# Second attention: even maxima with a row for two heads at a time, and one value product over high and low parts of the context keys

## The chip, the cores and the metric

The kernel runs on one core of a Trainium2 chip. Its engines are TensorE (PE in the rows; PEld is its loading of weights), VectorE (DVE), ScalarE (ACT), GpSimd (POOL) and SyncE (SP), which here issues nearly all transfers. They run side by side and wait for one another by semaphores. The metric is the device time of one execution in microseconds (us).

## The reference

Two layers run one after the other. The change lies in the attention of the second, in which 512 tokens of a batch (four batches) attend to the same 512 tokens and to 64 keys of a context. Cut to what matters:

```python
h = jnp.concatenate([x, latents], axis=1)            # x: 64 context tokens, latents: 512 tokens
q = (latents @ q_w + q_b).reshape(b, 512, 16, 32)
kv = (h @ kv_w + kv_b).reshape(b, 576, 16, 32, 2)
attn = jnp.einsum('bkhd,bnhd->bhkn', q, kv[..., 0]) / 32
attn = softmax(where(mask, attn, -inf))              # the mask concerns the 64 context keys
attn_out = jnp.einsum('bhkn,bnhd->bkhd', attn, kv[..., 1]) @ out_w + out_b + residual
```

All is float32. The kernel gets this precision from products of high and low parts: a number is split into a rounded high part and the rest, and three products (high by high, high by low, low by high) are added.

## The kernel before

A batch has 16 heads of 32 columns, in four groups of four (`c` is the group, `j` the head in it). The 576 keys of a head are five blocks: `t` 0 to 3 are 128 of the own tokens, `t` 4 (`TT`) is the 64 context keys. So a group has 20 steps (`NSTEP`), one for each (j, t) of `STEPS`, and a batch 80. In step n:

- TensorE multiplies keys by queries (`scores`, L2064) into one of two banks; the keys lie on the partitions, the 512 queries along them. Row 97 of the query stack (`ROWMAX`) holds the negative maximum of each query, so the product comes out with the maximum subtracted.
- ScalarE takes the exponential twice, once into the high part `ph` (L1156) and once in full into `pf` (L1157).
- VectorE or GpSimd (by `lo_by_pool`) writes the low part `pl` = pf - ph (L1331, `lo_p`, or L894).
- Four steps later (`LAG`), TensorE adds the values (`values`, L2079 with `ph` and L2080 with `pl`). The weights are 65 columns: 32 of high values, 32 of low values, one of ones for the sum.

The maxima must be known before a group's scores. TensorE computes the scores of the next group the other way round, queries on the partitions (`max_step`: L2042, or L2046 for the context keys, four small products), into one of two banks, and VectorE reduces each (L1570, L1573) before the bank is used again. `max_items(i)` says which of the 20 belong to step i: all within steps 2 to 15. At step 17 (`TURN`) VectorE joins the maxima of the group's four heads, TensorE turns them (L2053), VectorE copies the row out (L1586), and SP moves it to row 97 (`max_row`, L565). The next group's first scores wait for it (`maxed`).

Between the steps TensorE works off `fillers`: the projections of queries (Q), keys (K) and context keys (KC) of the group after next, and in group 1 also the turning of the next batch's tokens (T0 to T3, C). They and the turned maxima share two banks in a fixed order (`results`). SP moves the projected parts to memory and back into stacks (L546, L557). After step 79 comes a stretch of its own, with the values of the next batch's keys (`nV0` to `nV4`; `nV4` is the context), the sums' inverses and the output product (L2088). Before batch 0 comes a prologue that projects batch 0's values and takes the 20 maxima of its group 0 (`first_max`).

Of the kernel before, what the change touches and what calls it, by code (L numbers as in the profile page):

```python
# [26 lines left out]
F32 = mybir.dt.float32  # L27
# [8 lines left out]
P = 128  # L36
B, S, D = 4, 512, 512
C = 64
# [39 lines left out]
TURN = 17  # L78
OPEN_NORM = 4
# [24 lines left out]
def results(last):  # L104

    out = []
    for c in range(G):
        turn = [(TURN + 0.5, 1, f"R{c + 1}")] if c + 1 < G else [] if last else [(TURN + 0.5, 1, "nR0")]
        out += [u for _, _, u in sorted(fillers(c, last) + turn)]
# [5 lines left out]
         + [f"nV{t}" for t in range(TT)] + ["nR0", f"nV{TT}"])  # L115


def first_max(t, part):

    at = 2 * t + part  # L120
    return range((5 * at + 1) // 2, (5 * (at + 1) + 1) // 2)
# [57 lines left out]
def lo_by_pool(i):  # L179

    j, t = STEPS[i % NSTEP]
    return t in (1, 3) or (t == TT and j % 2 == 0)
# [27 lines left out]
def program(nc, x, ctx, mask_bool, mask_int, w, x1, xm, x2, q_parts, k_parts, out):  # L210
# [4 lines left out]
    with es:  # L215
# [41 lines left out]
        nT = rows_[0:H, 0:2 * P].rearrange("p (s n) -> p s n", s=2)  # L257
# [13 lines left out]
        pl = pl_.rearrange("p (r n) -> p r n", r=PRING)  # L271
        AS = [t[:, 0:TT * KT * P].rearrange("p (r k n) -> p r k n", r=TT, k=KT) for t in (ph_, pl_)]
# [66 lines left out]
        maxed = [sem("maxed0"), sem("maxed1")]  # L339
# [121 lines left out]
        def _(sp):  # L461
# [77 lines left out]
            def attention1():  # L539
# [31 lines left out]
                def batch(b, last):  # L571
# [14 lines left out]
                    for c in range(G):  # L586
# [5 lines left out]
                        def pair(half, xs=(0, 1)):  # L592
                            wait_apart(sp, (s_full, at(0, b, BSTEP, NSTEP * c + 2 * (TT + 1) * (half + 1))))
                            stack(nb, nc_, half, xs)
                        if last and c == G - 1:

                            wait_apart(sp, (pb_full, at(0, b, USES, use1(f"R{G - 1}", last) + 1)),
# [5 lines left out]
                        if c == 2 and not last:  # L603
                            wait_apart(sp, (pb_full, at(0, b, USES, use1(f"nT{KT - 1}") + 1)))
                            residual(b)
                        if ahead:
                            wait_apart(sp, (pb_free, at(0, b, USES, use1(f"{pre}Q{nc_}", last) + 1)))
                            parts(0, nb, nc_)
                        sums(HG * c)
                        if ahead:  # L610
                            pair(0, (0,))
                            wait_apart(sp, (pb_free, at(0, b, USES, use1(f"{pre}KC{nc_}", last) + 1)))
# [1660 lines left out]
```

## Time and profile before

| What | Value |
|---|---|
| median of 3 runs | 1783.35 us (1782.95 to 1785.82) |
| profiled execution, its time | 1778.49 us |
| its span | 1776.7 us |
| PE busy in the span | 1605.4 us (90%) |
| PEld busy | 1202.6 us (68%) |
| DVE busy | 1003.3 us (56%) |
| ACT busy | 688.9 us (39%) |
| POOL busy | 544.1 us (31%) |

The span is what the profiler saw of the program; the execution's own time is 1.8 us longer. Shares of busy time are averages over stages with different limits. A matmul's record is longer than the time after which the next one starts, so costs of TensorE are read here from the distance between two starts.

### The profile page before, as it was taken

Reading aid. Unit: us, or ns where it says so; the run is one execution under the profiler, and the core shown is the slowest. Engines: PE = TensorE matmul, PEld = TensorE weight load, DVE = VectorE, ACT = ScalarE, POOL = GpSimd, SP = SyncE. Lnnn points to the kernel's source line nnn. Section 1 sums busy time; section 2 is a strip of 40 time slices with the busy share of each in tenths; the row PEclk is TensorE's granted clock in tenths of the full one; section 3 lists DMA queues with packets and bytes.
Section 4 is the critical chain, followed back from the end, with each engine's and each line's share of the span. In section 5 each row is a group of like instructions: output and inputs, shape, how many; then the busy total and the mean of one; then the engine's idle time right before and its main releaser. Section 6 shows DMA issues by size and latency. Waiting matters only on the chain.

```text
span 1776.7 us, 23169 instructions
## 1 busy us (share of the span) xinstructions
PE 1605.4 (90%) x7017; PEld 1202.6 (68%) x7017; DVE 1003.3 (56%) x1625; ACT 688.9 (39%) x1243; POOL 544.1 (31%) x543
## 2 busy tenths in 40 slices
PE   5778787899999999798998999899988899999998
PEld 4667676667787787566666566566653677787886
DVE  4665656564333333487857776786788574333333
ACT  3533333341111112176737755773777432111111
POOL 3231236502122231343513432342358311303000
PEclk9888998999999999898999999999897999999999
DMA  5001104500010032522312322332221510101011
GB/s 185 1 33 54 45 28 138 207 13 31 18 30 18 24 133 83 183 77 96 100 59 97 113 67 85 91 101 63 99 88 48 192 52 16 33 12 36 0 48 47
DMA packets 60410, 126.18 MB, mean 71 GB/s; under 512 B 9989, under 2 KB 10378, under 8 KB 60322
## 3 DMA queue, kind: packets, MB, share of 16 engines
q1 hardware_dynamic: 53282, 102.13, 17.4%
q0 software_dynamic: 7040, 23.07, 4.1%
q8 instruction: 31, 0.51, 0.1%
q14 instruction: 57, 0.47, 0.1%
HBM read 90.25 MB, written 34.60 MB: 70 GB/s over the span
## 4 chain that ended last, share of the span: by engine, by line
PE 72%; DVE 13%; issue 7%; ACT 5%; DMA 1%; SPq 1%; POOL 1%; DVEq 0%; ACTq 0%; POOLq 0%
PE bank L2181 19%; PE bank L2193 18%; PE bank L2029 5%; DVE RA L1331 4%; PE bank L2025 3%; PE bank L2079 3%; DVE FA L1570 3%; PE bank L2064 3%; PE bank L2080 3%; PE bank L2088 3%; PE bank L2042 2%; PE bank L1827 2%; PE bank L1851 2%; PE bank L2046 2%; PE bank L1902 1%
## 5 line engine op out<-in xcount | busy, mean ns | idle before, releaser
L2193 PE MATMUL bank<-W,RA 128*128 128x512 f32 x1536 | 378.1, 397 | 6.0 <-DVE RA L1331 5.6
L2181 PE MATMUL bank<-RA,W 128*128 (+1 forms) x1536 | 374.8, 396 | 2.9 <-issue 2.4
L2193 PEld LDWEIGHTS bank<-W,RA 128*128 128x128 f32 x1536 | 286.2, 188 | 77.6 <-DVE RA L1331 10.0
L2181 PEld LDWEIGHTS bank<-RA,W 128*128 128x128 f32 x1536 | 286.9, 188 | 75.1 <-issue 6.1
L894 POOL TENSOR_TENSOR RA<-FA,RA 128x512 fp32r<-128x512 f32 (+1 forms) x160 | 216.6, 1358 | 373.0 <-ACT FA L1157 372.7
L1223 ACT ACTIVATE FA<-bank,cols 128x512 f32<-128x512 f32 x128 | 88.2, 689 | 540.8 <-PE bank L2181 540.7
L1331 DVE TENSOR_TENSOR RA<-FA,RA 128x512 fp32r<-128x512 f32 (+1 forms) x292 | 260.8, 893 | 33.2 <-ACT FA L1157 25.9
L1729 DVE CAST RA<-FA 128x512 fp32r<-128x512 f32 x128 | 62.8, 490 | 357.3 <-ACT FA L1223 357.3
L1156 ACT ACTIVATE RA<-bank 128x512 fp32r<-128x512 f32 (+1 forms) x320 | 193.3, 604 | 165.0 <-PE bank L2064 162.7
L1570 DVE TENSOR_REDUCE FA<-bank 128x1 f32<-128x512 f32 x256 | 168.9, 685 | 63.4 <-PE bank L2042 62.5
L1157 ACT ACTIVATE FA<-bank 128x512 f32<-128x512 f32 (+1 forms) x320 | 192.7, 602 | 0.0
L2064 PE MATMUL bank<-RA 98*128 98x512 f32 (+1 forms) x320 | 139.6, 438 | 9.6 <-ACT FA L1157 5.1
L2079 PE MATMUL bank<-RA 128*65 128x512 f32 (+1 forms) x320 | 138.5, 433 | 7.9 <-DVE RA L1331 4.9
L2029 PE MATMUL bank<-RA,W 128*128 128x512 f32 (+1 forms) x576 | 140.8, 361 | 1.9 <-DVE RA L1331 1.6
L1331 DVE TENSOR_TENSOR RA<-bank,RA 128x512 fp32r<-128x512 f32 (+1 forms) x124 | 83.0, 680 | 95.1 <-ACT RA L951 33.0
L2080 PE MATMUL bank<-RA 128*65 128x512 f32 (+1 forms) x320 | 132.9, 415 | 0.0
L2029 PEld LDWEIGHTS bank<-RA,W 128*128 128x128 f32 x576 | 95.0, 191 | 36.3 <-issue 12.2
L753 POOL TENSOR_TENSOR W<-raw,W 128x512 fp32r<-128x512 f32 (+1 forms) x88 | 108.3, 1231 | 7.3
L2042 PE MATMUL bank<-RA 97*128 97x512 f32 x256 | 96.6, 416 | 13.7 <-issue 6.5
L1764 DVE TENSOR_TENSOR FA<-bank,FA 128x512 f32 (+1 forms) x128 | 86.8, 690 | 38.3 <-PE bank L2193 37.7
L2064 PEld LDWEIGHTS bank<-RA 98*128 98x128 f32 (+1 forms) x320 | 59.3, 185 | 57.1 <-ACT FA L1157 32.6
L749 POOL TENSOR_SCALAR W<-raw 128x512 fp32r<-128x512 f32 (+1 forms) x88 | 57.8, 657 | 109.8 <-PE bank L2193 51.5
(154 smaller groups left out, 1810.2 us busy)
## 6 DMA issues: line engine op xcount, KB each, us to landing
RA<-k_parts SPq DMA_DIRECT2D x96, 144.0 KB
FA<-after_layer SPq DMA_DIRECT2D x12, 1024.0 KB, 5.9
RA<-q_parts SPq DMA_DIRECT2D x96, 128.0 KB
k_parts<-FA SPq DMA_DIRECT2D x16, 576.0 KB, 2.8
after_att<-FA SPq DMA_DIRECT2D x32, 256.0 KB, 2.1
q_parts<-FA SPq DMA_DIRECT2D x16, 512.0 KB, 2.7
raw<-in_L_xattn_mlp_w_dram POOLq DMA_DIRECT2D x32, 256.0 KB, 3.4
RA<-after_att SPq DMA_DIRECT2D x10, 512.0 KB, 7.1
```

The lines of the kernel that those rows point to most:

```text
L894: pool.tensor_tensor(pl[0:m, r, :], pf[0:m, r, :], ph[0:m, r, :].bitcast(F32), ALU.subtract).then_inc(p_lo_pool, 1)
L1156: act.activation(ph[0:m, r, :], src, ACT.Exp, scale=SCALE1)
L1157: act.activation(pf[0:m, r, :], src, ACT.Exp, scale=SCALE1).then_inc(p_exp, 1)
L1331: dve.tensor_tensor(dst, src, hi.bitcast(F32), ALU.subtract).then_inc(sem_, 1)
L1570: dve.tensor_reduce(nm_main[:, TT * j + t:TT * j + t + 1], bank[2 + i % 2][:, :], AX_X, ALU.max, negate=True).then_inc(mm_free, 1)
L2029: op = pe.matmul(dst[:, 0:m], W[:, "QK".index(kind[0]), a, k, c * P:(c + 1) * P], src[:, d, k, :], start=start, stop=stop)
L2042: pe.matmul(bank[2 + i % 2][:, :], QS[0:ROWMAX, c % 2, j, t * P:(t + 1) * P], KS[0:ROWMAX, c % 2, j, 0:S], start=True, stop=True).then_inc ...
L2064: pe.matmul(bank[4 + n % 2][0:m, :], KS[0:ROWMAX + 1, c % 2, j, t * P:t * P + m], QS[0:ROWMAX + 1, c % 2, j, :], start=True, stop=True).th ...
L2079: pe.matmul(o, v, ph[0:m, n % PRING, :], start=(t == 0), stop=False)
L2080: pe.matmul(o, v, pl[0:m, n % PRING, :], start=False, stop=(t == TT)).then_inc(pv_step, 1)
L2181: op = pe.matmul(bank[FC1_BANK[i]][:, :], W[:, slot, a, k, i * P:(i + 1) * P], yT_[:, ds(b * (2 * KT * S) + (d * KT + k) * S, S)], start=( ...
L2193: op = pe.matmul(bank[4 + t][:, :], gs[:, a, i, t * P:(t + 1) * P], W[:, slot + 1, d, i, :], start=(i == 0 and a == 0 and d == 0), stop=(i ...
```

## The change

- **Maxima.** Each step now takes one item: steps 0 to 6 (`SHIFT` is 7) the last seven of the own group, steps 7 to 19 the first thirteen of the next. The row is turned, copied and moved in two halves, each for two heads: heads 0 and 1 at step 17 of the group before, heads 2 and 3 at step 7 of the own group. The first scores of head 0 wait for the one and those of head 2 (step 10) for the other. The last batch's group 2 takes two items a step from step 7 to 16, since group 3 has none. The prologue takes 13 items instead of 20.
- **Fillers.** Q now lies in steps 0 to 5, K in 8 to 13 and KC in 14 and 15 (in group 1: Q 0 to 2, K 3 to 5, KC 8, T at 9, 11, 13 and 15, C at 18).
- **Context values.** The low part of the context's exponentials goes to partitions 64 to 127 of the same slot of `ph` (`lo_place`), and the context's value weights stand twice, on partitions 0 to 63 and 64 to 127. One product over 128 partitions takes the place of two over 64. ScalarE and VectorE have one more instruction each for `nV4`.
- **Who writes low parts.** GpSimd now has t 1 and 3 and, for even heads, t 0 instead of the context block.

```diff
+SHIFT = 7
-def max_items(i):
-    return range(max(i - 2, 0) * 10 // 7, min(max(i - 1, 0) * 10 // 7, NSTEP)) if i < 16 else range(0)
+def max_items(c, i, last):
+    if last and c == G - 1:
+        return []
+    if i < SHIFT:
+        return [(c, NSTEP - SHIFT + i)]
+    if last and c == G - 2:
+        return [(c + 1, 2 * (i - SHIFT) + m) for m in range(2)] if i < TURN else []
+    return [(c + 1, i - SHIFT)]
+def max_turns(c, last):
+    if last and c == G - 1:
+        return {}
+    if last and c == G - 2:
+        return {SHIFT: (c, 1), (SHIFT + TURN) // 2: (c + 1, 0), TURN: (c + 1, 1)}
+    return {SHIFT: (c, 1), TURN: (c + 1, 0)}
...
-    spans = ((1, 5), (6, 5), (11, 1)) if turns else ((1, 6), (7, 5), (12, 1))
+    spans = ((0, 3), (3, 3), (8, 1)) if turns else ((0, 6), (8, 6), (14, 2))
...
-        plan += [(s0, 1, f"nT{k}") for k, s0 in enumerate((12, 13, 15, 18))] + [(19, 1, "nC")]
+        plan += [(s0, 1, f"nT{k}") for k, s0 in enumerate((9, 11, 13, 15))] + [(18, 1, "nC")]
...
-    return t in (1, 3) or (t == TT and j % 2 == 0)
+    return t in (1, 3) or (t == 0 and j % 2 == 0)
...
+        def lo_place(n):
+            return ph[C:P, n % PRING, :] if STEPS[n % NSTEP][1] == TT else pl[:, n % PRING, :]
...
-                def max_row(nb, c):
-                    sp.dma_start(QS[ROWMAX:ROWMAX + 1, c % 2, :, :].rearrange("o j (q n) -> o (j q) n", n=P).bitcast(F32),
-                                 nT[:, c % 2, :].bitcast(F32)).then_inc(maxed[c % 2], 16)
+                def max_row(c, pair):
+                    sp.dma_start(QS[ROWMAX:ROWMAX + 1, c % 2, 2 * pair:2 * pair + 2, :]
+                                 .rearrange("o j (q n) -> o (j q) n", n=P).bitcast(F32),
+                                 nT[:, c % 2, pair, :].bitcast(F32)).then_inc(maxed[c % 2][pair], 16)
...
+                        if t == TT:
+                            act.activation(VP[C:P, t, :, 0:HD], src, ACT.Copy)
...
+                        if t == TT:
+                            dve.tensor_tensor(VP[C:P, t, :, HD:2 * HD], values_, hi_.bitcast(F32), ALU.subtract)
...
-                        if i == 0:
-                            wait_apart(pe, (maxed[c % 2], at(0, b, 32, 16 * (c // 2 + 1))))
+                        if t == 0 and j % 2 == 0:
+                            wait_apart(pe, (maxed[c % 2][j // 2], at(0, b, 32, 16 * (c // 2 + 1))))
...
-                        v = VP[0:m, t, h, 0:2 * HD + 1]
+                        v = VP[:, t, h, 0:2 * HD + 1]
                         o = bank[6 + h % 2][0:2 * HD + 1, :]
-                        pe.matmul(o, v, ph[0:m, n % PRING, :], start=(t == 0), stop=False)
-                        pe.matmul(o, v, pl[0:m, n % PRING, :], start=False, stop=(t == TT)).then_inc(pv_step, 1)
+                        op = pe.matmul(o, v, ph[:, n % PRING, :], start=(t == 0), stop=(t == TT))
+                        if t < TT:
+                            op = pe.matmul(o, v, pl[:, n % PRING, :], start=False, stop=False)
+                        op.then_inc(pv_step, 1)
```

Two places show what moves. The first is TensorE's queue at step 8 of group 0 in the loop over batches 0 to 2. Before, the step has scores (128x512 under L2064), two items of maxima (L2042 and, for the context, four of L2046), the context's values as two products (L2079 and L2080, 65 rows out), and two products of the K filler (L2029):

```order
L2064 MATMUL bank<-RA 128x512
L2040 REGISTER_ALU
L2042 MATMUL bank<-RA 128x512
L2040 REGISTER_ALU
L2046 MATMUL bank<-RA 128x64 x4
L2074 REGISTER_ALU
L2079 MATMUL bank<-RA 65x512
L2080 MATMUL bank<-RA 65x512
L2029 MATMUL bank<-RA,W 128x512 x2
```

In the changed kernel the lines are L2113 (scores), L2090 (maxima), L2127 (values), L2077 (fillers), and L2101 the turning of eight rows of maxima, at the end of step 7:

```order
L2101 MATMUL bank<-ident,FA 8x128
L2111 REGISTER_ALU
L2113 MATMUL bank<-RA 128x512
L2088 REGISTER_ALU
L2090 MATMUL bank<-RA 128x512
L2127 MATMUL bank<-RA 65x512
L2040 REGISTER_ALU
L2077 MATMUL bank<-RA,W 128x512 x2
```

One item of maxima is left in the step, one product in place of two stands for the context's values, and a turning stands ahead of it.

The second place is SP's queue in the same loop, group 0, from the parts of the keys (L546 before) to the row of maxima (L565 before, `RA<-rows_`). Before, a sum (L576) and its wait lie between them:

```order
L546 DMA k_parts<-FA 128x1152
L573 REGISTER_ALU
L576 DMA FA<-FA 1x16x32
L454 REGISTER_ALU
L565 DMA RA<-rows_ 1x16x128
L557 DMA RA<-k_parts 32x2x576 x3
```

Now (L575 the parts, L594 the row, L586 the stack) the half row of step 17 follows the parts at once, since KC ends at step 15 and its parts are ready only then:

```order
L575 DMA k_parts<-FA 128x1152
L483 REGISTER_ALU
L594 DMA RA<-rows_ 1x8x128
L586 DMA RA<-k_parts 32x2x576 x3
```

The row went from behind the sum to right behind the parts of the keys.

## Rows read from the trace of the kernel before

**Rows 1.** Windows of batch 1: groups 0 to 3, then the stretch behind them
```profile
core 0: us, PE busy (x) PEld busy (x) DVE busy (x) ACT busy (x) POOL busy (x), PEclk, DMA share, GB/s
916.45:947.75 31.30, 27.23 (x122) 17.79 (x121) 24.70 (x37) 22.56 (x45) 12.84 (x10) 1.00 0.28 96
947.75:984.66 36.91, 32.67 (x150) 22.21 (x150) 27.21 (x42) 25.92 (x52) 13.83 (x11) 0.95 0.25 76
984.66:1015.92 31.26, 29.09 (x129) 18.90 (x130) 26.56 (x41) 24.28 (x49) 12.99 (x11) 1.00 0.41 124
1015.92:1047.18 31.26, 29.33 (x131) 19.41 (x132) 25.97 (x39) 24.02 (x49) 18.50 (x14) 1.00 0.29 89
1047.18:1080.59 33.41, 31.85 (x129) 21.83 (x128) 17.74 (x24) 7.57 (x13) 2.60 (x2) 1.00 0.21 63
```

**Rows 2.** Windows: prologue's maxima, group 0 of batch 3, group 2 of batch 3
```profile
727.01:747.00 19.99, 18.32 (x79) 14.05 (x77) 12.67 (x22) 1.80 (x3) 4.01 (x5) 0.92 0.47 142
...
1244.62:1277.48 32.86, 29.71 (x122) 19.58 (x121) 24.69 (x37) 22.72 (x45) 12.70 (x10) 0.88 0.26 90
...
1310.10:1340.71 30.61, 25.72 (x93) 14.63 (x94) 24.80 (x36) 23.00 (x46) 24.34 (x24) 0.89 0.31 86
```

**Rows 3.** TensorE's waits in the four batches: us in total, times, longest
```profile
PE bank L2046 <- DVE FA L1570: 22.2, 27, 1.9
PE bank L2006 <- DVE FA L1560: 8.0, 6, 1.6
PE bank L2064 <- DMA RA<-rows_: 4.2, 9, 0.7
```

**Rows 4.** Timeline of TensorE, batch 1, group 0: start, us, instruction [idle before]
```profile
924.06 0.53 PE L2046 MATMUL bank<-RA 97*128 97x64 f32 x4
924.42 0.42 PE L2079 MATMUL bank<-RA 128*65 128x512 f32 x1
...
925.38 0.39 PE L2064 MATMUL bank<-RA 98*128 98x512 f32 x1
...
927.00 0.40 PE L2064 MATMUL bank<-RA 98*128 98x512 f32 x1
...
937.45 1.42 PE L2029 MATMUL bank<-RA,W 128*128 128x64 f32 x12
938.70 0.48 PE L2064 MATMUL bank<-RA 98*128 98x512 f32 x1
939.02 0.64 PE L2042 MATMUL bank<-RA 97*128 97x512 f32 x2
939.59 0.44 PE L2079 MATMUL bank<-RA 64*65 64x512 f32 x1
...
940.18 0.45 PE L2064 MATMUL bank<-RA 98*64 98x512 f32 x1
...
945.01 0.27 PE L2053 MATMUL bank<-ident,FA 128*16 128x128 f32 x1
...
947.75 0.48 PE L2064 MATMUL bank<-RA 98*128 98x512 f32 x1 [0.52 <-DMA RA<-rows_]
```

**Rows 5.** Low parts in batch 1: count, duration in ns min/median/max, span, forms
```profile
L1331 DVE TENSOR_TENSOR RA<-FA,RA x39: 673/723/1773, 919.9 to 1045.9; 128x512 fp32r<-128x512 f32 x32, 64x512 fp32r<-64x512 f32 x7
...
L894 POOL TENSOR_TENSOR RA<-FA,RA x39: 1267/1287/1817, 919.4 to 1045.1; 128x512 fp32r<-128x512 f32 x31, 64x512 fp32r<-64x512 f32 x8
```

**Rows 6.** Transfers: issuer, count, KB each, median us from issue to landing
```profile
k_parts<-FA SPq DMA_DIRECT2D x16, 576.0 KB, 2.8
...
RA<-rows_ SPq DMA_DIRECT2D x22, 8.0 KB, 1.8
```

**Rows 7.** Timeline of the stretch behind batch 1's groups: context values, output
```profile
1067.76 0.59 ACT L1137 ACTIVATE RA<-bank 64x512 fp32r<-64x512 f32 x1 [0.64 <-PE bank L2025]
1068.38 0.68 DVE L1331 TENSOR_TENSOR RA<-bank,RA 64x512 fp32r<-64x512 f32 x1 [0.48 <-ACT RA L1137]
...
1069.31 11.45 PE L2088 MATMUL bank<-W,RA 128*128 128x512 f32 x48 [0.61 <-DVE RA L1331]
```

More of the change, by code:

```diff
@@ L107, in results @@
     for c in range(G):
-        turn = [(TURN + 0.5, 1, f"R{c + 1}")] if c + 1 < G else [] if last else [(TURN + 0.5, 1, "nR0")]
+        turn = [(i + 0.5, 1, turn_name(*of)) for i, of in max_turns(c, last).items()]
         out += [u for _, _, u in sorted(fillers(c, last) + turn)]
@@ L338, in program @@
         stacked = [[sem(f"stacked{i}_{j}") for j in range(2)] for i in range(2)]
-        maxed = [sem("maxed0"), sem("maxed1")]
+        maxed = [[sem(f"maxed{i}_{a}") for a in range(2)] for i in range(2)]
         mm_full = sem("mm_full")
@@ L609, in batch @@
                         sums(HG * c)
+                        if (SHIFT + TURN) // 2 in turned:
+                            turned_row((SHIFT + TURN) // 2)
                         if ahead:
                             pair(0, (0,))
+                        sums(HG * c + 1)
+                        if ahead:
                             wait_apart(sp, (pb_free, at(0, b, USES, use1(f"{pre}KC{nc_}", last) + 1)))
                             parts(1, nb, nc_)
[L614 to L618 removed]
+                        if TURN in turned:
+                            turned_row(TURN)
                         if ahead:
@@ L1633, in batch @@
                         at_step = {s0 + n + 1: u for s0, n, u in fillers(c, last)}
-                        ahead = not (last and c == G - 1)
-                        nb, nc_ = (b, c + 1) if c + 1 < G else (b + 1, 0)
+                        turns = max_turns(c, last)
                         for i in range(NSTEP):
                             n = NSTEP * c + i
-                            if ahead:
-                                for m in max_items(i):
-                                    max_step(nb, nc_, m)
-                                if i == TURN - 1:
-                                    max_join(nb, nc_)
+                            for of, m in max_items(c, i, last):
+                                max_step(b + of // G, of % G, m)
+                            if i + 1 in turns:
+                                of, pair = turns[i + 1]
+                                max_join(b + of // G, of % G, pair)
                             lo_p(n - 1)
@@ L1645, in batch @@
                                 lo(b, at_step[i], last)
-                            if ahead and i == TURN:
-                                max_turned(b, f"R{nc_}" if c + 1 < G else "nR0", nb, nc_, last)
+                            if i in turns:
+                                of, pair = turns[i]
+                                max_turned(b, turn_name(of, pair), b + of // G, of % G, pair, last)
                             h, t = divmod(n - LAG - 2, TT + 1)
@@ L1705, in attention1 @@
                         dve.memset(VP[:, :, :, 2 * HD:VW].bitcast(F32), 1.0).then_inc(consts, 1)
-                for t in range(TT):
+                for t in range(TT - 1):
                     for i in first_max(t, 0):
@@ L1712, in attention1 @@
                         max_step(0, 0, i)
-                max_join(0, 0)
+                max_join(0, 0, 0)
+                lo(0, f"nV{TT - 2}", first=True)
+                max_turned(0, "nR00", 0, 0, 0, first=True)
+                for part in range(2):
+                    for i in first_max(TT - 1, part):
+                        max_step(0, 0, i)
                 lo(0, f"nV{TT - 1}", first=True)
-                max_turned(0, "nR0", 0, 0, first=True)
                 lo(0, f"nV{TT}", first=True)
@@ L2107, in batch @@
                         at_step = {s0 + part: (u, part, n) for s0, n, u in fillers(c, last) for part in range(n)}
-                        ahead = not (last and c == G - 1)
-                        nb, nc_ = (b, c + 1) if c + 1 < G else (b + 1, 0)
+                        turns = max_turns(c, last)
                         for i in range(NSTEP):
                             scores(NSTEP * c + i)
-                            if ahead:
-                                for m in max_items(i):
-                                    max_step(nb, nc_, m)
+                            for of, m in max_items(c, i, last):
+                                max_step(b + of // G, of % G, m)
                             if NSTEP * c + i >= LAG:
@@ L2119, in batch @@
                                 project(b, u, part, n, last)
-                            if not ahead and i >= 17:
+                            if last and c == G - 1 and i >= 17:
                                 spread_inverse(i - 17)
-                            if ahead and i == TURN:
-                                max_turn(b, f"R{nc_}" if c + 1 < G else "nR0", nb, nc_, last)
+                            if i in turns:
+                                of, pair = turns[i]
+                                max_turn(b, turn_name(of, pair), b + of // G, of % G, pair, last)
                     values(BSTEP - 4)
```

58 lines of the change are left out of this document (33 added, 25 removed).

## The prediction

> **What bounds the kernel now.** I read the windows first, cut where each group's first scores start. An ordinary group of 20 steps takes 31.3 us, group 1, which also turns the next batch's tokens, 36.9, and the stretch behind the groups 33.4 [rows 1]. In the windows of the groups TensorE is the busiest engine, but VectorE is close behind it, with 24.7 to 27.2 us; ScalarE has 22.6 to 25.9 and GpSimd 12.8 to 18.5. Since a matmul's record overlaps the next, I then took TensorE's own need from distances between starts [rows 4]:
>
> - A product over 512 columns: from the scores at 925.38 to those at 927.00 lie seven, 1.62 us, so 0.232 each.
> - The four small products of a context maximum: 924.06 to 924.42, 0.36. KC's twelve: 937.45 to 938.70, 1.25. The turned row: 0.27.
> - The context's two value products: two full products start at 939.02 and should end the stretch after 0.46, but the next starts at 939.59, so 0.11 are lost at the change to 64 rows; then 0.59 pass to 940.18. Together 0.70 us for what 128 rows would do in 0.46.
>
> An ordinary group has 92 full products (20 scores, 16 maxima, 32 of values, 24 fillers), 21.3 us, and 4 x 0.36 + 4 x 0.70 + 1.25 + 0.27 = 5.8: 27.1 us. It takes 31.3, so TensorE stands still for 4.2. The list of waits says for what: mostly for a bank of maxima that VectorE has not reduced (22.2 us in 27 waits over the four batches), in group 1 for the bank in which a filler is turned (8.0), and for the row (4.2) [rows 3]. So the stage is bound by TensorE, plus bunched maxima: up to two items in a step for which VectorE must find time between low parts, and none in steps 16 to 19. The chain of waits is alternately TensorE and VectorE for that reason, and neither is idle long.
>
> **The change, part by part.**
>
> *One product for the context values.* It takes 0.232 instead of 0.70, so 0.47 less a head, 1.9 a group, and TensorE's need falls from 27.1 to 25.3; the second turned row brings it to 25.5. For the other bound: if what costs at 64 rows did not vanish with the form, only one product of 0.232 would go, 0.9 a group.
>
> The Trainium skill ("TensorE: Matmul & The Clock Gate", section "Why this matters for your kernels") says that a product over few rows takes the same time as one over 128. By that rule the gain would be the one product, 0.23 a head. The trace disagrees so far: 0.59 us for two.
>
> *Even maxima.* They take nothing off any engine; they remove waits. VectorE's need stays what it was, about 25 to 26.5 us a group, since busy times of 24.7 to 26.6 [rows 1] hold the same instructions, and a second joining and copying add about 0.4. With one item a step, steps with a filler need on TensorE 6 x 0.232 = 1.39 and the six without one (6, 7, 16 to 19) 0.93, where VectorE needs its average of about 1.3. The sum is TensorE's 25.5 plus 6 x 0.37 = 2.2, or 27.7. Not all low parts are alike: one on VectorE takes 0.67 at best and 1.77 at worst, beside GpSimd's 1.29 [rows 5], so a step is now and then late; I add 0.7. And the rows, next, 0.6. An ordinary group then takes 29.0 us, 2.3 less than now. The bounds of this: 26.3 (TensorE's need and 0.8 of waits) and 30.5 (VectorE as slow as now in three of four waits).
>
> *The row in two halves.* From the turning at 945.01 to the scores at 947.75 pass 2.74 us, of which TensorE waited 0.52 [rows 4]; the transfer is 1.8 of them [rows 6]. At step 17 nothing changes in this path but its neighbours: SP now issues the 576 KB of key parts right ahead of the row, and these land after 2.8 us [rows 6]. If a transfer waits for the one in front of it, the row lands about 0.5 to 0.9 later; if not, as now. Steps 18 and 19 give 1.6 us of TensorE's own work and about 2.5 at VectorE's pace, so about the present 0.5 is waited again. The half of step 7 has steps 8 and 9 with fillers in front of it, 2.55 us or more, so 0 to 0.5. No row found here stands behind a large transfer, so both ends stay for the range. What stands behind the waiting scores is all of TensorE's queue, but VectorE catches up meanwhile, so a wait is not lost whole. I take 0.6 a group for both, 0.5 of which it pays now; the other 0.1 is in the sum.
>
> *Group 1.* Its 36.9 us contain waits for the bank of a turned filler, 1.3 us each on average [rows 3]. K now ends at step 5 and the turnings come at every second step, one use behind the other. Its need is 25.5 plus five turnings of about 0.45, 27.8; with the same additions (eight light steps, 3.0; 1.3 for late steps and rows) 32.1, and I take 32.4 for what is left of bank waits: 4.5 less, three times, 13.5.
>
> *Batch 3.* Groups 0 and 1 are both ordinary there; group 0 takes 32.9 at a granted clock of 0.88 [rows 2], and I take group 1 for its like. I take 3 less for each, 6. Group 2 now has 27 items instead of 20, with two a step in ten steps. It has no fillers and TensorE is not its bound; seven more reductions at 0.6, of which two thirds find room: 1.5 more (0 to 3).
>
> *Prologue.* Twenty maxima and four value projections take 20.0 us [rows 2]. Seven items fewer, each worth about 0.45 on the path (its product, and VectorE's 0.6 where it is waited for): 3 less.
>
> *Context values in weights.* Behind the groups, ScalarE's 0.59 and VectorE's 0.68 for `nV4` are in the path: the output product starts at 1069.31 after waiting 0.61 for just this low part [rows 7]. One more of each, at about 0.5 and 0.6 between starts, moves it by 1.1, and what follows on VectorE (the last scaling) by as much: 3 x 1.1 = 3.3 slower, with nothing to hide it. The last head's context product also lies in this stretch: 4 x 0.47 = 1.9 faster.
>
> *Who writes low parts.* GpSimd has ten a group as before and VectorE ten; nothing on the path.
>
> *Sum.* Nine ordinary groups 20.7, three groups 1 13.5, batch 3 6 - 1.5, prologue 3, the stretches 1.9 - 3.3: 40.3 us faster. The profiled execution's 1778.5 becomes 1738.2; the median of the runs lies 4.9 above that execution, so I forecast 1743.
>
> **The rivals.**
>
> *VectorE and GpSimd become the bound.* A low part on VectorE reads two operands from memory, as GpSimd's does, and its spread from 0.67 to 1.77 [rows 5] looks like one waiting for the other. GpSimd's 12.8 us [rows 1] stay the same while the group gets shorter, so more of VectorE's low parts meet it. Then a group takes 30.2, 1.1 less, group 1 gains 2.5, batch 3 3: 10 + 7.5 + 3 - 1.5 + 2 - 1.4 = 20, 1763. For it speaks that VectorE's 26.6 and TensorE's 25.5 would change places; against it, that VectorE's waits for maxima (the bunching) go too. Chance 0.19.
>
> The Trainium skill ("SBUF — State Buffer", section "SBUF: two separate sides") has this as a rule: the two engines share a pair of ports under an exclusive lock for a whole instruction. By that rule the time would be this rival's.
>
> *The product saves only a product.* 0.23 instead of 0.47 a head: 64 x 0.24 = 15 less gained, 1758. Chance 0.08.
>
> *Waits vanish whole.* Groups at 26.5, 4.8 less, group 1 at 29.5: nine by 2.5 and three by 2.9 more than in my sum, 31 in all, 1712. Against it: light steps are too short for VectorE. Chance 0.08.
>
> *Slower: the rows stand in TensorE's way.* There are now two row paths a group, each of at least 2.2 us from turning to landing, with only two steps to hide it. TensorE's turning also waits for VectorE's joining, in the middle of its queue. If VectorE is a step late (1.3) and the transfer sits behind the key parts (0.9), a half row costs 2 us more than I counted: 28 rows in the groups, 56 us, against 40: 1799. It decides from 1.5 us a row on. Against it: the present row waits 0.5 on average where it waits at all. Chance 0.05.
>
> **How the numbers follow.** My own case, from 1729 to 1757, has 0.60. Case by case: 0.60 at 1743, 0.19 at 1763, 0.08 at 1758, 0.08 at 1712, 0.05 at 1799. The range from 1719 to 1767 leaves out the slower case, most of the 1712 one and the upper edge of the VectorE rival, about 0.15 to 0.2. A measurement of this kernel tells about 0.2% (3.6 us) from no change. Faster by more than that: 0.93; within it: 0.02, from the upper end of the VectorE rival; slower: 0.05.
>
> **What would show it.** In the profile of the changed kernel: an ordinary group at 29 us and group 1 at 32 to 33; TensorE's waits for L1570's successor (L1613) down from 22 us to under 8, those on a filler's bank under 3; waits for the row 4 to 15 us in 20 or more waits; the context value product followed by the next after 0.23 to 0.25 us; the low part's spread as now; the output product about 1.1 us later behind the last `nV4` product; VectorE's busy share in a group near 90%. I am wrong if groups stay above 30.3, if row waits pass 30 us in total, or if waits for low parts in `values` appear.

## The result and the profile after

The changed kernel is slower: 1795.01 us median of 7 runs (1790.78 to 1802.12) against 1781.76 us (1777.9 to 1785.82), a ratio of 1.0083 with a 95% interval of 1.0065 to 1.0101. The forecast, 1743 us and faster, was wrong in sign. The profiled execution took 1798.13 us with a span of 1796.3.

In the changed kernel the scores are L2113, the own maxima L2090 (reduced in L1613), the turning L2101, the joining L1623, the copying of the row L1630, its transfer L594, the values L2127 and L2129, the fillers L2077, the low parts L1372 and L933, the output product L2138. The windows of batch 1, cut as in [rows 1], then group 0 of batch 3 as in [rows 2] and group 1 behind it:

```profile
914.17:946.65 32.48, 26.80 (x121) 18.78 (x119) 22.61 (x39) 23.68 (x46) 13.78 (x10) 0.94 0.26 92
946.65:982.59 35.94, 32.88 (x147) 23.49 (x147) 27.09 (x45) 25.08 (x50) 13.59 (x10) 0.88 0.25 80
982.59:1016.85 34.26, 28.68 (x127) 20.27 (x127) 25.74 (x43) 25.05 (x50) 13.83 (x10) 0.94 0.33 111
1016.85:1048.30 31.45, 28.57 (x127) 20.26 (x128) 24.70 (x40) 23.21 (x45) 17.94 (x14) 0.95 0.23 71
1048.30:1084.75 36.45, 33.36 (x131) 23.19 (x128) 19.88 (x27) 8.25 (x14) 1.73 (x1) 0.95 0.23 74
1256.04:1284.91 28.87, 25.02 (x121) 17.80 (x119) 22.42 (x39) 23.55 (x46) 13.84 (x10) 0.98 0.27 99
1284.91:1321.90 36.99, 30.79 (x126) 21.83 (x127) 25.60 (x41) 24.36 (x47) 13.88 (x10) 0.87 0.24 77
```

Batch 1 takes 170.6 us where it took 164.1. Of these windows only group 0 of batch 3 is at the forecast 29; there the clock is 0.98. In every window of batch 1 the granted clock lies below that of before. Over the four batches (first scores to last) it is 0.92 instead of 0.96. TensorE's waits in the same stretch as [rows 3], us in total, times, longest:

```profile
PE bank L2113 <- DMA RA<-rows_: 20.5, 8, 3.3
PE bank L2101 <- DVE FA L1623: 16.5, 16, 1.3
PE bank L2077 <- DVE FA L1598: 9.3, 11, 1.9
PE bank L2127 <- POOL RA L933: 6.1, 2, 3.8
PE bank L2138 <- DVE RA L1372: 5.7, 3, 1.9
PE bank L2090 <- DVE FA L1613: 4.4, 4, 1.6
```

Most of the waits for bunched maxima are gone, 22.2 us to 4.4 (and 2.9 more for the context's maxima, L1616). In their place stand two that the kernel before hardly had: the row, 4.2 to 20.5 us, in few but long waits, and VectorE's joining, in front of the turning. All eight row waits are for a half row of step 17: seven at the start of groups 1 and 3, one at that of group 2 of batch 3. Right ahead of each lies a group that has KC in steps 14 and 15, and so the key parts just ahead of the row on SP's queue. The half rows of step 7 are not waited for. Both waits are to be seen at the end of batch 1's group 0, in the timeline of all engines (start, us, instruction, [idle before]):

```profile
938.59 0.69 DVE L1372 TENSOR_TENSOR RA<-FA,RA 64x512 fp32r<-64x512 f32 x1
...
940.09 0.68 DVE L1646 TENSOR_TENSOR FA<-bank,FA 32x512 f32<-32x512 f32 x1
...
940.67 1.26 POOL L933 TENSOR_TENSOR RA<-FA,RA 128x512 fp32r<-128x512 f32 x1 [3.09 <-ACT FA L1198]
940.81 0.42 DVE L1616 TENSOR_REDUCE FA<-bank 128x4 f32<-128x256 f32 x1
...
941.27 0.69 DVE L1623 TENSOR_TENSOR FA<-FA 128x8 f32<-128x8 f32 x1
941.88 0.68 DVE L1372 TENSOR_TENSOR RA<-FA,RA 128x512 fp32r<-128x512 f32 x1
...
942.11 0.27 PE L2101 MATMUL bank<-ident,FA 128*8 128x128 f32 x1 [1.12 <-DVE FA L1623]
...
943.28 0.27 DVE L1630 CAST rows_<-bank 8x128 fp32r<-8x128 f32 x1
...
943.60 0.35 SPq L575 DMA_DIRECT2D k_parts<-FA  x1
...
944.14 0.73 SPq L594 DMA_DIRECT2D RA<-rows_  x1
...
946.65 0.77 PE L2113 MATMUL bank<-RA 98*128 98x512 f32 x1 [2.47 <-DMA RA<-rows_]
```

VectorE comes to the joining with a low part (938.59, the context block's), a K part, a head's sum (L1646) and a context maximum in front of it, without a pause between them; the joining itself, 8 columns, takes 0.69 us, and ends just when GpSimd's low part does (940.67 and 1.26). TensorE waits 1.12. Then SP issues the key parts ahead of the row, and TensorE waits 2.47 more, from turning to scores 4.5 us. Behind that wait it runs at half the clock (0.54 granted from 946.65 to 953.47), as its own timeline shows:

```profile
947.64 0.63 PE L2127 MATMUL bank<-RA 128*65 128x512 f32 x1
948.06 0.63 PE L2129 MATMUL bank<-RA 128*65 128x512 f32 x1
...
953.47 0.40 PE L2113 MATMUL bank<-RA 98*128 98x512 f32 x1
953.70 0.40 PE L2090 MATMUL bank<-RA 97*128 97x512 f32 x1
```

From 947.64 on products follow each other after 0.42 us, from 953.47 on after 0.23. So a wait of 2.5 us costs an estimated 3 us more in the 6.8 behind it: what TensorE did there in 6.8 us, it would do in about 3.8 at 0.23. The other seven row waits are followed by a low clock too: in the 7 us behind the eight it is 0.54 to 0.76.

### The profile page after: what moved, and what is told of

Same layout as the page of the kernel before. It is cut to its first block, busy times and chain, and to the rows that moved or that the text cites. A ratio compares the mean times of both kernels' runs of the same rounds, so it can differ in the third digit from the quotient of the medians.

```text
span 1796.3 us, 23219 instructions
## 1 busy us (share of the span) xinstructions
PE 1598.9 (89%) x6969; PEld 1220.3 (68%) x6969; DVE 994.8 (55%) x1661; ACT 692.3 (39%) x1247; POOL 548.2 (31%) x543
## 4 chain that ended last, share of the span: by engine, by line
PE 68%; DVE 15%; issue 8%; ACT 5%; DMA 2%; POOL 1%; DVEq 0%; SPq 0%; ACTq 0%; POOLq 0%
PE bank L2231 19%; PE bank L2243 18%; PE bank L2077 6%; DVE RA L1372 4%; PE bank L2113 3%; PE bank L2138 3%; PE bank L2073 2%; PE bank L2127 2%; PE bank L2090 2%; PE bank L1875 2%; PE bank L2129 2%; PE bank L1899 2%; DVE FA L1613 2%; PE bank L1950 1%; DVE FA L1646 1%
## 5 line engine op out<-in xcount | busy, mean ns | idle before, releaser
L933 POOL TENSOR_TENSOR RA<-FA,RA 128x512 fp32r<-128x512 f32 x160 | 219.9, 1376 | 387.7 <-ACT FA L1198 387.2
L2231 PEld LDWEIGHTS bank<-RA,W 128*128 128x128 f32 x1536 | 286.9, 188 | 75.0 <-issue 6.1
L1613 DVE TENSOR_REDUCE FA<-bank 128x1 f32<-128x512 f32 x256 | 173.6, 684 | 111.1 <-PE bank L2090 106.1
L1372 DVE TENSOR_TENSOR RA<-FA,RA 128x512 fp32r<-128x512 f32 (+1 forms) x292 | 227.2, 778 | 11.6 <-ACT FA L1198 3.1
L2113 PE MATMUL bank<-RA 98*128 98x512 f32 (+1 forms) x320 | 145.5, 455 | 24.4 <-DMA RA<-rows_ 20.5
L2077 PE MATMUL bank<-RA,W 128*128 128x512 f32 (+1 forms) x576 | 150.3, 376 | 12.1 <-DVE FA L1598 9.3
L2127 PE MATMUL bank<-RA 128*65 128x512 f32 x320 | 139.1, 435 | 8.9 <-POOL RA L933 6.1
L2077 PEld LDWEIGHTS bank<-RA,W 128*128 128x128 f32 x576 | 104.4, 203 | 48.0 <-DVE FA L1598 14.6
L1372 DVE TENSOR_TENSOR RA<-bank,RA 128x512 fp32r<-128x512 f32 (+1 forms) x124 | 82.9, 680 | 82.3 <-ACT RA L990 33.0
L2090 PE MATMUL bank<-RA 97*128 97x512 f32 x256 | 108.7, 430 | 14.0 <-issue 6.4
L2129 PE MATMUL bank<-RA 128*65 128x512 f32 x256 | 110.1, 430 | 0.0
L2113 PEld LDWEIGHTS bank<-RA 98*128 98x128 f32 (+1 forms) x320 | 62.1, 194 | 59.1 <-issue 28.7
```

The lines of the kernel that those rows point to most:

```text
L933: pool.tensor_tensor(lo_place(n), pf[0:m, r, :], ph[0:m, r, :].bitcast(F32), ALU.subtract).then_inc(p_lo_pool, 1)
L1372: dve.tensor_tensor(dst, src, hi.bitcast(F32), ALU.subtract).then_inc(sem_, 1)
L1613: dve.tensor_reduce(nm_main[:, TT * j + t:TT * j + t + 1], bank[2 + i % 2][:, :], AX_X, ALU.max, negate=True).then_inc(mm_free, 1)
L2077: op = pe.matmul(dst[:, 0:m], W[:, "QK".index(kind[0]), a, k, c * P:(c + 1) * P], src[:, d, k, :], start=start, stop=stop)
L2090: pe.matmul(bank[2 + i % 2][:, :], QS[0:ROWMAX, c % 2, j, t * P:(t + 1) * P], KS[0:ROWMAX, c % 2, j, 0:S], start=True, stop=True).then_inc ...
L2113: pe.matmul(bank[4 + n % 2][0:m, :], KS[0:ROWMAX + 1, c % 2, j, t * P:t * P + m], QS[0:ROWMAX + 1, c % 2, j, :], start=True, stop=True).th ...
```

## The experiments

All ratios are to the kernel before, in runs of the same chip. The chip is one for e1 to e4 and e12, a second for e5 to e8 and a third for e9 to e11, so a difference between rows of different chips carries the intervals of both.

| Experiment | Median, us | Ratio, 95% interval |
|---|---|---|
| e1: product, new division, old maxima | 1780.4 | 0.999, 0.9972 to 1.0008 |
| e2: even maxima, old products, old division | 1758.85 | 0.9858, 0.9829 to 0.9887 |
| e3: the change with the row first | 1777.75 | 0.9962, 0.9945 to 0.9978 |
| e4: the change, turnings a step earlier | 1819.17 | 1.021, 1.0177 to 1.0244 |
| e5: the change with the old division | 1767.51 | 0.9936, 0.9913 to 0.9958 |
| e6: e5 with the row first | 1749.29 | 0.9821, 0.9785 to 0.9857 |
| e7: e2 with the new division | 1781.93 | 1.0004, 0.9981 to 1.0026 |
| e8: before with the new division alone | 1789.38 | 1.0051, 1.0032 to 1.007 |
| e9: e6, context's values projected third | 1748.35 | 0.983, 0.9811 to 0.985 |
| e10: e2 with the row first | 1737.99 | 0.9773, 0.9758 to 0.9788 |
| e11: before with the product, old division | 1781.83 | 1.0007, 0.9988 to 1.0027 |
| e12: e6, second copies of weights made late | 1734.78 | 0.9731, 0.9717 to 0.9744 |

"Division" is `lo_by_pool`, which engine writes which low parts.

### e1 and e2: the two halves of the change

e1 is the kernel before with the one product, its doubled weights and the new division of low parts; e2 the changed kernel with this taken back:

```diff
-    return t in (1, 3) or (t == 0 and j % 2 == 0)
+    return t in (1, 3) or (t == TT and j % 2 == 0)
...
-                        op = pe.matmul(o, v, ph[:, n % PRING, :], start=(t == 0), stop=(t == TT))
-                        if t < TT:
-                            op = pe.matmul(o, v, pl[:, n % PRING, :], start=False, stop=False)
+                        pe.matmul(o, v, ph[0:m, n % PRING, :], start=(t == 0), stop=False)
+                        pe.matmul(o, v, pl[0:m, n % PRING, :], start=False, stop=(t == TT)).then_inc(pv_step, 1)
```

> The kernel before with the context's single value product, its doubled weights and the new division of low parts alone; maxima, rows and fillers as before. If the changed kernel's loss comes from the paths of the two half rows, the product is a gain of its own: 60 heads at up to 0.47 us, less 3 us for the doubled weights, 0.985 to 0.995 of before. If VectorE and GpSimd set the pace, TensorE's saving is waited away: 0.998 to 1.002.

> The changed kernel with the two old context products and the old division of low parts: even maxima, half rows and new filler places alone. Rows theory: the loss is all here, 1.015 to 1.025 of before, and the waits for rows and for the joined maxima stay at some 37 us. VectorE theory: the loss has its root in low parts, so it is below 1.008.

The even maxima alone gain 1.4%, some 25 us. Product and new division alone give nothing, and on top of the even maxima they cost 2.3% (1.0083 against 0.9858). Of e2's two theories the rows theory (1.015 to 1.025) falls; the other said only below 1.008, and neither named a gain. In e2 the joining comes without delay, and the turning (L2097) without a wait:

```profile
931.15 0.68 DVE L1642 TENSOR_TENSOR FA<-bank,FA 32x512 f32<-32x512 f32 x1
931.87 0.42 DVE L1612 TENSOR_REDUCE FA<-bank 128x4 f32<-128x256 f32 x1
932.33 0.17 DVE L1619 TENSOR_TENSOR FA<-FA 128x8 f32<-128x8 f32 x1
...
932.73 0.27 PE L2097 MATMUL bank<-ident,FA 128*8 128x128 f32 x1
```

Its row waits, 18.5 us in 10, are as long as the changed kernel's. So they belong to the even maxima, and are paid there out of a larger gain.

### e3 and e4: the row

e3 lets SP issue the row of step 17 ahead of the key parts; e4 turns both halves one step earlier, and moves the fillers with them:

```diff
                        sums(HG * c + 1)
+                        if TURN in turned:
+                            turned_row(TURN)
                         if ahead:
                             wait_apart(sp, (pb_free, at(0, b, USES, use1(f"{pre}KC{nc_}", last) + 1)))
                             parts(1, nb, nc_)
-                        if TURN in turned:
-                            turned_row(TURN)
```

> The changed kernel, but SP moves the half row of step 17 first and the parts of the keys after it. If the row waits behind the 576 KB, it lands in 1.8 us instead of 2.5 in ten groups, and TensorE's waits for rows (20.5 us) fall to 10 to 14: 5 to 15 us less than the changed kernel, 1.000 to 1.006 of before. If the transfer ahead does not matter, the same as the changed kernel, 1.008.

> The changed kernel with both turnings a step earlier (16 and 6 for 17 and 7) and the fillers moved ahead to fit. Rows theory: each half row has a step more, 1.2 to 1.4 us, so the waits of 2.5 us shrink to 1 or so and the clock falls behind them partly go too: 0.985 to 0.998 of before. VectorE theory: it still takes its 25 to 27 us a group and is late at the joining all the same: 1.005 to 1.010.

e3 gains 1.2% over the change, more than expected, and later e6 over e5 as much. Row waits fall from 20.5 to 11.7 us, longest 1.4; the 8.8 are less than half of the 21 us gained. The clock tells of the rest: 0.94 over the four batches instead of 0.92. In the 7 us behind each of e3's nine row waits the granted clock is 1.00, with one exception (0.76), where the changed kernel had 0.54 to 0.76 behind all eight. Taking 7 x (1 - clock) as lost behind each, that is 19 us in the changed kernel and 2 in e3, an estimate that with the 8.8 is more than the gain. e4 was worse than either of its theories had it, 1.021. Its waits for fillers and for maxima grew:

```profile
PE bank L2077 <- DVE FA L1598: 22.6, 11, 2.7
PE bank L2090 <- DVE FA L1613: 18.2, 20, 2.1
PE bank L2113 <- DMA RA<-rows_: 11.9, 8, 2.3
```

The row waits fall here too, but fillers wait longer for their bank (9.3 to 22.6 us), and maxima again for VectorE (4.4 to 18.2). Two things were changed at once, so e4 tells nothing on an earlier row by itself.

### e5 to e8: who writes the low parts

e5 and e6 give GpSimd the context block of even heads again, with the one product kept (GpSimd waits for its own low part ahead of and behind that block, since it now lies in the high part's buffer); e7 and e8 change only the division, in e2 and in the kernel before:

```diff
-    return t in (1, 3) or (t == TT and j % 2 == 0)
+    return t in (1, 3) or (t == 0 and j % 2 == 0)
```

> The changed kernel with the old division of low parts alone restored: GpSimd again has the context block of even heads and VectorE their t 0; the context's single product stays, and GpSimd waits for itself before and behind the block that it moves to partitions 64 to 127. Division theory (VectorE has low parts in two steps running just ahead of each joining): the waits for the joined maxima go from 16.5 us to next to none and the time falls under that of the maxima alone, 0.975 to 0.988 of before. Product theory (what costs comes with the product itself, by the doubled weights or a faster TensorE): 1.003 to 1.010.

> As the run above, and the half row of step 17 moved ahead of the key parts. Rows theory: the row waits of some 18 us fall to 10 and the clock falls behind them get fewer, 5 to 15 us less than the run above, 0.968 to 0.982 of before. If the row's place in SP's queue only mattered because VectorE was late: the same as the run above.

> Even maxima and half rows with the two old context products, but with the new division of low parts. Division theory: 1.005 to 1.020 of before, and joined maxima are waited for 12 to 20 us. Product theory: as the maxima alone, 0.983 to 0.989.

> The kernel before with the new division of low parts alone. Division theory: also slower here, 1.003 to 1.012, since the product alone gave nothing (0.999) where its own saving should have given up to 1%. Product theory, or a division that only hurts beside even maxima: 0.998 to 1.002.

The new division costs 1.5% with even maxima, with the product (1.0083 against 0.9936) as without it (1.0004 against 0.9858), and 0.5% in the old order. e5 and e7 both came out between the ranges of their two theories: the waits for the joining did what the division theory said, and the time moved by less. These waits are 16.5 us in the changed kernel and 12.9 in e7, against none listed in e2 and 4.0 in e5 (three, each behind a joining that took 1.18 us beside GpSimd); e7's rows:

```profile
PE bank L2109 <- DMA RA<-rows_: 16.7, 8, 3.0
PE bank L2097 <- DVE FA L1619: 12.9, 12, 1.3
```

Both divisions give VectorE ten low parts a group. The new one lays two of them side by side at steps 4 and 5 and at 14 and 15 (the context block of an even head and t 0 of the next); the old one at 9 and 10 and at 19 and 0. The joinings are at steps 7 and 17. In VectorE's queue the first of a new pair, the context's block, comes ahead of the joining and the second right behind it (938.59 and 941.88 above). In e2 GpSimd has that block, and VectorE stood idle for 0.92 us ahead of the same joining. So one low part more stands in front, and it makes VectorE late enough to meet GpSimd: without its 0.69 us the joining would have started before GpSimd's low part at 940.67, an estimate. The meeting stretches it; its durations (ns, min/median/max) in the changed kernel, and then in e2:

```profile
L1623 DVE TENSOR_TENSOR FA<-FA x31: 166/697/1294, 756.4 to 1356.1; 128x8 f32<-128x8 f32 x31
```

```profile
L1619 DVE TENSOR_TENSOR FA<-FA x32: 166/168/1276, 740.3 to 1317.7; 128x8 f32<-128x8 f32 x32
```

The Trainium skill ("SBUF — State Buffer", section "SBUF: two separate sides") says that a VectorE instruction with two inputs from SBUF and a GpSimd instruction that reads SBUF shut each other out for a whole instruction. The trace agrees: the joining ended at 941.96, GpSimd's low part at 941.93; and in e2 GpSimd's low part, begun 0.10 us after one of VectorE's, took 1.73 us instead of 1.27. Of the 31 joinings of the changed kernel 20 took 0.6 us or more, each beside a low part of GpSimd and over when that was; the other 11 took 0.17. TensorE stood idle ahead of the turning behind 19 of the 20, and behind one of the 11. In the place shown the stretch is 0.52 of the 1.12 us waited (0.69 less 0.17). How the 1.5% as a whole divides between the low part in front, the stretch and the clock behind the waits was not taken apart.

### e9 to e12: the product's own account

e11 puts the product alone into the kernel before, with the old division; e10 is e2 with the row first, to stand against e6. e9 and e12 try to mend the stretch behind the groups. e9 projects `nV4` third of five. e12 copies the second weights from memory, behind the engines' last work for the output product:

```diff
-                        if t == TT:
-                            dve.tensor_tensor(VP[C:P, t, :, HD:2 * HD], values_, hi_.bitcast(F32), ALU.subtract)
                         split_lo(VP[0:m, t, :, HD:2 * HD], values_, hi_, pb_free)
...
                         as_lo_(3)
+                        lo_again(b)
...
+                def lo_again(b, first=False):
+                    dve.wait_ge(pb_free, at(0, b, USES, use1("nV4", False, first) + 1))
+                    dve.tensor_copy(VP[C:P, TT, :, HD:2 * HD], VP[0:C, TT, :, HD:2 * HD].bitcast(F32)).then_inc(v_again, 1)
```

> The version with the product, the even maxima, the old division of low parts and the row first, with the context's value projection (nV4, whose two products by ScalarE and two by VectorE stand in front of the output product) made third of five instead of last. Theory A, the doubled weights sit on the path that ends the stretch behind the groups: the output product's wait goes from 1.9 back to 0.6 us, three times, and where the wait cost half the clock too, up to 1.5 more each; 4 to 8 us, so the ratio goes from 0.982 to 0.977 to 0.980. Theory B, VectorE's whole work in that stretch is what takes longer: the wait only moves to the place of the third projection, the output product starts as late as before, and the ratio stays at 0.982.

> Even maxima with the row ahead of the key parts on SP's queue, old context products, old division; nothing of the value product. It stands against 0.982, which the same has with the product. Row first has given 1.2% twice. Theory A, the product costs more in the tail (about 2.6 us a batch) than it saves in the groups: 0.974 to 0.979 here. Theory B, the product is a gain once rows no longer wait: 0.985 to 0.988 here, since 0.986 without the row first would hardly change.

> The kernel before with the value product alone, the division of low parts as before, so GpSimd writes the context's low parts of every second head straight into the lower half of the high part's buffer. Theory A, product and division add up: 0.994 (0.999 with both, over 1.005 for the division alone), about 11 us faster, a third of the 27 that I had counted for the product. Theory B, the old division hides behind the old order anyhow and the product gives nothing: 0.998 to 1.001.

> As e6 (product, even maxima, old division, row first, projections in the old order), but the second copies of the context's value weights are made later and from memory instead of from the bank: ScalarE copies the high part to the upper 64 rows behind its last work for the output product, VectorE the low part likewise, so that the bank of nV4 is free after one product of each again. Theory A, the doubled weights in front of the output product are half of what the stretch behind the groups lost (38.3 us against 35.1 without the product): the output product waits 0.6 us instead of 1.9, the stretch takes 36.8 to 37.2, and the whole ratio is 0.978 to 0.980, still behind the 0.977 of the kernel without the product, since the wait of 1.0 us for the reciprocals and the piece at half the clock behind it stay. Theory B, the stretch is as long as VectorE's work in it, which is still there: 0.982.

In the old order the product gives nothing (e11), against the 0.6% that e1 and e8 had promised by subtraction, each with 0.2% to either side. TensorE waits for maxima there for 24.9 us in 35 waits, against 22.2 in 27 [rows 3]: part of what the product saves, it waits for VectorE. It also waits 8.5 us instead of 5.1 for ScalarE in front of scores, and 5.7 instead of 1.9 for the output product. With even maxima the product costs 0.5% (e6 against e10, each interval 0.15 to 0.36% to either side). The windows of batch 1 tell where; first e10, then e6 (here the last group ends at its step 79, and the last row is the stretch from there to the next batch):

```profile
900.52:929.54 29.02, 26.30 (x123) 17.84 (x122) 21.51 (x39) 23.52 (x46) 14.07 (x10) 1.00 0.25 84
929.54:961.50 31.96, 30.72 (x150) 20.80 (x151) 25.25 (x45) 25.30 (x52) 14.74 (x11) 1.00 0.28 88
961.50:992.53 31.03, 29.77 (x130) 20.08 (x131) 23.48 (x42) 24.96 (x49) 14.37 (x11) 0.95 0.38 125
992.53:1019.69 27.16, 27.10 (x126) 18.38 (x126) 22.10 (x39) 22.38 (x45) 17.50 (x13) 1.00 0.32 102
1019.69:1054.76 35.07, 33.37 (x135) 22.80 (x135) 20.66 (x28) 8.50 (x14) 3.18 (x3) 1.00 0.23 77
```

```profile
902.90:933.13 30.23, 26.53 (x120) 18.83 (x119) 21.62 (x39) 23.57 (x46) 14.34 (x10) 0.94 0.24 81
...
996.47:1022.05 25.58, 25.22 (x122) 18.34 (x123) 21.95 (x36) 21.84 (x43) 17.56 (x13) 1.00 0.34 108
1022.05:1060.33 38.28, 34.49 (x134) 23.77 (x134) 21.77 (x31) 9.45 (x16) 3.64 (x3) 0.96 0.22 70
```

Group 3 is 1.6 us shorter with the product, at full clock in both, near the 1.9 (4 x 0.47) of my sum. The stretch behind it is 3.2 longer. (The batch as a whole is 3.2 longer too: groups 0 and 1 are 1.2 and 0.9 longer, at a clock of 0.94 instead of 1.00, and group 2 is 0.6 shorter.) What is in those 3.2 the timeline of e6 shows (L2153 spreads the inverses, L2077 is a projection of values, L2142 the output product):

```profile
1031.39 1.09 PE L2153 MATMUL bank<-FA,rows_ 12*128 12x512 f32 x2 [1.00 <-DVE FA L1659]
1032.41 4.49 PE L2077 MATMUL bank<-W,RA 128*128 128x512 f32 x12
...
1049.03 11.47 PE L2142 MATMUL bank<-W,RA 128*128 128x512 f32 x48 [1.92 <-DVE RA L1376]
```

TensorE comes to the inverses earlier than VectorE and waits 1.00 for them; the twelve products behind that wait take 4.49 instead of 3.06, in part at half the clock again (0.64 granted in that stretch); and the output product waits 1.92 for the second low part instead of 0.61 [rows 7]. e9 moved that last wait and didn't remove it, in front of another projection, which again takes 4.60 us instead of 3.06:

```profile
1038.00 4.60 PE L2077 MATMUL bank<-W,RA 128*128 128x512 f32 x12 [1.76 <-DVE RA L1376]
...
1048.90 11.47 PE L2142 MATMUL bank<-W,RA 128*128 128x512 f32 x48 [0.63 <-DVE RA L1376]
```

Its expectation called this theory B, and its ratio is e6's. In e12 the wait is gone:

```profile
1026.22 1.09 PE L2162 MATMUL bank<-FA,rows_ 12*128 12x512 f32 x2 [0.97 <-DVE FA L1666]
1027.24 4.61 PE L2086 MATMUL bank<-W,RA 128*128 128x512 f32 x12
...
1042.66 11.47 PE L2151 MATMUL bank<-W,RA 128*128 128x512 f32 x48 [0.61 <-DVE RA L1381]
```

The wait at the inverses is still there. The stretches of batches 0 to 2 take 35.5, 37.1 and 35.5 us, where e6 had 38.4, 38.3 and 38.1: 6.6 us together. The ratio fell by more than I expected of it, from 0.9821 to 0.9731 (16 us; 13.6 in the spans of the profiled executions). The rest lies mostly in the groups behind those stretches (in batch 1, group 0 takes 28.5 instead of 30.2, at a clock of 1.00 instead of 0.94) and in batch 3; why, was not tried apart. e12 is the fastest version here, 2.7% ahead of the kernel before. It is also 0.4% ahead of e10, which has no product, but on another chip, and their spans differ by only 2 us (1733.0 and 1735.0). Nothing waits for the new semaphore `v_again` itself: TensorE's first use of the copies stands behind its waits for later work of the same two engines.

## Why the prediction was wrong

**What the parts add up to.** With the old division and the row first the same change is at 0.9821 (e6), and with the second copies late at 0.9731 (e12). My forecast of 1743 us is a ratio of about 0.978. So the sum was reached only where the terms that I had put at nothing or too low were taken out of the kernel.

**What bounds the kernel.** Right in part. TensorE's need and the bunched maxima were read rightly. But "neither is idle long" hid that VectorE has no room just where TensorE waits for it; e11 shows that in the old order 0.47 us less per head on TensorE gives nothing.

**Who writes low parts.** This is the step that failed: "GpSimd has ten a group as before and VectorE ten; nothing on the path." It is on the path, with 1.5%, about 27 us, the largest single cost of the change (e7 against e2, the changed kernel against e5). I had counted instructions, and not looked at which steps they stand in. In the order of instructions one low part more of VectorE now stands ahead of each joining, for which TensorE waits in the middle of its queue, and the later joining mostly runs into a low part of GpSimd.

**Even maxima.** The mechanism was right: waits for maxima fell to 4.4 us (I had said under 8), and alone the step is worth 25 us (e2). Of my sum of 40.3, 25 were the product's (1.9 in each of 14 groups, 1.9 for the last heads, less 3.3), so 15 were left for the maxima: too little by 10. The prologue was sized nearly right: the first scores come at 747.1 instead of 751.4, 4.3 us earlier, where I had said 3.

**The row.** This step failed as well. Both ends had been kept, 0 and 0.5 to 0.9 late behind the key parts, but priced at 0.6 a group; measured it was about 1.0 late (waits of 2.45 against 1.43 in e3), half of it because SP issues the row 0.54 later. Waits for the row were 20.5 us in all, outside my 4 to 15, and in 8 waits instead of 20 or more. And they brought a granted clock of 0.54 to 0.76 in the 7 us behind them, which no term had. My sum took the clock of the kernel before for granted. With the row first the gain was 1.2%, 21 us (e3), and again 1.15% (e6 against e5); both times the row waits in the list fell by less than 9. My rival on the slower side said 1799 by this mechanism ("VectorE is a step late" and "the transfer sits behind the key parts"), and gave it 0.05. Its two conditions are what the trace shows at 941 and at 943.6; its place was right, though not its price for each row, since only some rows wait, and the clock pays the rest.

**The context's product.** The single product costs what I said, about 0.23 to the next: from 989.44 to 989.67 in

```profile
989.44 0.39 PE L2127 MATMUL bank<-RA 128*65 128x512 f32 x1
989.67 0.62 PE L2077 MATMUL bank<-RA,W 128*128 128x512 f32 x2
```

and group 3 of e6 is 1.6 us shorter than that of e10, so the rival that it saves only a product (0.9 a group) falls. But as a whole it came to nothing in the old order, and with even maxima to a loss of 0.5%. The term that was mis-sized is the stretch behind the groups: I had said 1.1 a batch, and it was 3.2 (1.3 for the output product's wait, 1.0 for the inverses and 1.4 of half clock, less what TensorE was ahead). With the copies off the path the product is worth 2 us by the spans and 0.4% or 8 us by the ratios (e12 against e10, two chips), not 25.

**Group 1 and batch 3.** Group 1 was to take 32.4 and took 35.9; with the old division and the row first it takes 32.9 (e6). Group 0 of batch 3 went from 32.9 to 28.9 as forecast, at a clock of 0.98, but group 1, which I took for its like, took 37.0, at a clock of 0.87. A row wait of 2.46 stands right ahead of it and one of 3.32 at its end, and both its turnings wait 1.0 behind stretched joinings. In e6 that group takes 28.2 at full clock. Group 2, where I had said 1.5 more, went from 30.6 to 36.3 (33.7 in e6); there TensorE waits 3.8 us for one low part of GpSimd.

**VectorE and GpSimd as the bound** (1763) doesn't hold as I put it. VectorE was busy 22.6 of 32.5 us in group 0, less than before. Not its share was full, but the stretch of its queue ahead of each joining.

## What to carry to other kernels

When an engine is close to the one that bounds, what counts is not how much work it has in a group but what stands in its queue right ahead of the instruction that the other waits for; a reassignment that keeps the counts can cost 1.5%. Read the order of instructions there before pricing an edit at nothing. A small transfer for which TensorE waits belongs ahead of a large one on the same queue, and a wait of TensorE has to be priced with the half clock behind it. And a second copy of weights can be made from memory once the bank is handed back, not in front of the engine that waits for the bank.

## What the hardware showed unexpectedly

- Waits of TensorE of 1 to 3.3 us were followed by some 3 to 7 us at half the clock (1.2 GHz instead of 2.4), in a stage where it was otherwise busy: after 2.47 us products came every 0.42 us until 953.47; after 1.00 us twelve products took 4.49 instead of 3.06. Not each wait did so. Behind row waits, in the 7 us that follow: all eight of the changed kernel (2.44 to 3.32) were followed by a clock of 0.54 to 0.76; of the eight in e2 of 2.0 or more six were, and two by 1.00; of e6's eleven none was, ten of 0.84 to 1.45 and one of 2.42. The output product behind 1.91 us in the changed kernel took 12.99 instead of 11.45, and behind 1.92 us in batch 1 of e6 it took 11.47 (in batch 0 of the same run 12.99); in e5 the same wait for the inverses (0.98 us) slowed nothing. What decides between them stays open, and with it a part of every sum here. The row of the changed kernel:

```profile
1071.92 12.99 PE L2138 MATMUL bank<-W,RA 128*128 128x512 f32 x48 [1.91 <-DVE RA L1372]
```

- An instruction of VectorE on 8 columns took 0.17 us alone and 0.69 (up to 1.29) beside GpSimd, and ended with GpSimd's.
- A row of 4 KB issued 0.54 us behind the 576 KB of key parts let the scores start 2.51 us later (944.14 to 946.65); issued ahead of them, 1.97 us later (e6, 931.16 to 933.13).
